# Expert picks on the logits, normed rows kept in place, the second bias on VectorE, alternating scatters, and one load for both results of a bin

## The chip, the cores and the metric

The kernel runs on one core of one Trainium2 chip. The metric is the device time of one execution in microseconds (us). Before the change the median of three runs is 2775.14 us (2773.34 to 2776.78).

## The reference, cut to what matters

Two layers, each added to its input, over 6250 nodes with 256 features, all in float32.

The graph layer norms the rows, builds one message for each of 100000 edges (two small products with a norm between them), sums the messages by source node and passes node and sum through two more products. The change does not touch its arithmetic.

The expert layer is what the change is about:

```python
tokens = layernorm(x)                                   # [6250, 256]
logits = tokens @ router_w.T                            # 8 experts
probs  = softmax(logits)
rw, re = top_k(probs, 2)
rw     = rw / max(rw.sum(-1), 1e-12)                    # two shares per token
for e in range(8):
    h   = gelu(tokens @ w1[e] + b1[e])
    y   = h @ w2[e] + b2[e]
    out = out + combine[:, e] * y                       # out starts as tokens
x = x + out
```

## The kernel before, in words

The nodes are cut into 50 bins of 126 rows (the last has 76). `node_rows` holds one bin per column block in SBUF: first the input, then the summed messages, then the running result. The program is a sequence of blocks, each of which gives every engine its own instruction list; a block ends when all engines have ended theirs.

- **nodes_and_sort** (to 600.5 us) norms the nodes, computes the products that do not depend on edges and sorts the edges. It zeroes `node_rows` on ScalarE (L564).
- **messages** (to 2151 us) goes over 838 tiles of 128 edges. The change touches it only in the shape of `node_rows` and by an instruction ahead of GpSimd's first one.
- A block between the two layers holds only GpSimd's `sem_clear` (L118).
- **update** (L1248) goes over the bins as a software pipeline written out by hand: a loop over steps `n` in every engine's list, in which an operation with lag `d` works on bin `n - d`. TensorE turns the sums of bin n (L1617), multiplies by `u1b` for bin n-2 (L1584), turns and multiplies again for bins n-3 and n-4, multiplies by the router for bin n-8 (L1605) and turns the normed row of bin n-7 (L1612). ScalarE copies the turned rows out of PSUM, applies Silu (L1539) and copies the logits last in its step (L1547). VectorE adds the u row (L1735), takes statistics (L1741, L1758), norms (L1751) into a ring `token` of 25 rows, adds xh (L1767) and adds token and x1 into `node_rows` (L1772). GpSimd makes the reciprocal deviation of one bin per step (`normal`, L1449, L1452). SyncE loads the u and xh rows four bins ahead (L1391, L1394) and, behind the fourth, both expert weights and the biases (L1397 to L1401).
- Routing goes by batches of five bins (the last two have three and two). In the step with lag 10 VectorE takes the batch's maximum and subtracts it (L1659, L1660) and ScalarE takes Exp (L1552); with lag 11 VectorE makes the softmax (L1667 to L1669) and the first pick (L1676 to L1684); with lag 12 the second pick, the counts (L1690, L1696) and the shares (L1705 to L1709); with lag 13 TensorE ranks (L1627, L1629); with lag 14 VectorE writes the places (L1719 to L1724). Then GpSimd scatters every normed row twice to the DRAM area `by_expert`, once for each pick: five `send` (L1464) for the first, in the five steps that follow, then five for the second. Each row carries the row number to which its result goes; GpSimd writes that number into `token` ahead of either half (`name_rows`, L1459), the second time after the first half has landed.
- **experts** (L1821) goes over 56 tiles of 256 scattered rows. TensorE's list has for each step the four transposes of tile n (L1940), the second product of tile n-4 into `ps_ye` and the first product of tile n-1. The second product is twice a bias matmul (`ones2` by `b2_parts`, two rows deep, L1953) and six matmuls (L1957). VectorE copies `ps_ye` out (L1989) and GpSimd scatters the two halves to `y_rows` (L1888). At the block's end GpSimd waits until all have landed.
- **combine** (L2016) is a block of its own: for each bin SyncE loads the two results with two transfers into a ring of eight bins (L2039), VectorE adds them with their shares into `node_rows` (L2055, L2062), ScalarE's queue stores the row (L2046).

What holds the order in the update, in a few lines (PE: the router's product; ScalarE; GpSimd's second half):

```python
pe.wait_ge(h2_t_ready, g + 1)
pe.wait_ge(l_kept, g)              # one PSUM buffer for the logits
product(ps_l[0:BIN, 0:E], h2_t[:, g % TURNED], rw).then_inc(l_ready, 1)

if i == size:
    pool.wait_ge(first_landed[b % 2], landed(b, 2))
    name_rows(b, 1)
```

Of the kernel before, what the change touches and what calls it, by code (L numbers as in the profile page):

```python
# [13 lines left out]
ds = bass.ds  # L14
# [37 lines left out]
ROUND = 1.5 * 2 ** 23  # L52

# [10 lines left out]
BATCHES = [(s, BATCH) for s in range(0, BINS - BATCH, BATCH)] + [(BINS - BATCH, 3), (BINS - 2, 2)]  # L64
HELD = 5 * BATCH
# [21 lines left out]
def gnn_ffn(nc, t, out):  # L87
    with ExitStack() as whole:
        whole.enter_context(nc.allow_non_contiguous_dma("small transposed parameters"))
        node_rows = whole.enter_context(nc.sbuf_tensor("node_rows", [P, BINS, D], F32))  # L90
# [8 lines left out]
        with ExitStack() as edges:  # L99
# [10 lines left out]
            messages(nc, dram, node_rows, ident, kept)  # L110
        dram["by_expert"] = nc.dram_tensor("by_expert", (EXPERTS * (REGION + MOE_TILE), XROW), F32).ap()
        dram["y_rows"] = nc.dram_tensor("y_rows", (2 * ROWS + 2 * EXPERTS * MOE_TILE, D), F32).ap()
        with ExitStack() as rest:
# [4 lines left out]
            with nc.Block() as block:  # L118
                @block.gpsimd
                def _(pool):  # L120

                    pool.sem_clear(range(used[0].num, used[-1].num + 1))

            tile_e = sb("tile_e", [1, MOE_TILES], I32)
            tile_off = sb("tile_off", [1, MOE_TILES], I32)
            with ExitStack() as weights:
# [8 lines left out]
                w["b2_parts"] = weights.enter_context(nc.sbuf_tensor("b2_parts", [2, EXPERTS, D], F32R))  # L135
                w["ones2"] = weights.enter_context(nc.sbuf_tensor("ones2", [2, P], F32R))
                update(nc, t, dram, node_rows, ident, w, shares, tile_e, tile_off)
                experts(nc, dram, ident, w, tile_e, tile_off)
            combine(nc, dram, node_rows, shares, out)


def nodes_and_sort(nc, t, dram, node_rows, ident, kept):
# [4 lines left out]
    with ExitStack() as ctx:  # L147
# [239 lines left out]
        def _(sp):  # L387
# [8 lines left out]
            sp.dma_start(node_rows[0:BIN, 0:BINS - 1, :],  # L396
                         t["x"][0:(BINS - 1) * BIN, :].rearrange("(b p) f -> p b f", p=BIN)).then_inc(x_in, 16)
            sp.wait_ge(last_clear, 1)
            sp.dma_start(node_rows[0:LAST, BINS - 1, :], t["x"][(BINS - 1) * BIN:, :]).then_inc(x_in, 16)
# [92 lines left out]
        def _(act):  # L492
# [71 lines left out]
            nc.scalar.activation(node_rows[:].rearrange("p b f -> p (b f)"), zero[:].broadcast_to([P, BINS * D]),  # L564
# [70 lines left out]
        def _(dve):  # L635
# [186 lines left out]
            for i in range(BINS):  # L822
                if i >= 2:
                    dve.wait_ge(means, i - 1)
                nc.vector.bn_stats(st6[0:BIN, i % 2, :], node_rows[0:BIN, i, :]).then_inc(stats, 1)
# [30 lines left out]
            def normed(i):  # L856
# [4 lines left out]
                nc.vector.tensor_scalar(h[0:BIN, i % 3, :], node_rows[0:BIN, i, :], mv[0:BIN, i, 0:1],  # L861
# [6 lines left out]
            for i in range(BINS):  # L868
# [7 lines left out]
                nc.vector.tensor_tensor(xh_out[0:BIN, k, :], h[0:BIN, i % 3, :], node_rows[0:BIN, i, :], ALU.add  # L876
# [69 lines left out]
def messages(nc, dram, node_rows, ident, kept):  # L946
# [6 lines left out]
    with ExitStack() as ctx:  # L953
# [72 lines left out]
        def _(pool):  # L1026
            nc.gpsimd.memset(half[:], -0.5).then_inc(start, 1)
# [146 lines left out]
        def _(dve):  # L1174
# [3 lines left out]
            def step(j, r, live):  # L1178
# [3 lines left out]
                def add_sums(i, d):  # L1182
# [4 lines left out]
                    sums = node_rows[0:BIN, ds(b[i], 1), :]  # L1187
# [60 lines left out]
def update(nc, t, dram, node_rows, ident, w, shares, tile_e, tile_off):  # L1248
# [5 lines left out]
    with ExitStack() as ctx:  # L1254
# [19 lines left out]
        token = sb("token", [P, HELD, XROW])  # L1274
        st6 = sb("st6_u", [P, R, 6])
        mv = sb("mv_u", [P, R, 2])
        rstd = sb("rstd_u", [P, R, 1])
        half = sb("half_u", [P, 1])
        blank = sb("blank", [P, E, 2, XROW])
        logits = sb("logits", [P, 2 * BATCH, E])  # L1280
# [6 lines left out]
        prob = sb("prob", [P, BATCH, E])  # L1287
        work = sb("work_r", [P, BATCH, E])
        low = sb("low", [P, BATCH])
        total = sb("total", [P, BATCH])  # L1290
        best = [sb("best0", [P, BATCH]), sb("best1", [P, BATCH])]
# [5 lines left out]
        b2 = sb("b2", [E, D])  # L1297
        b2_hi = sb("b2_hi", [E, D], F32R)
        b2_lo = sb("b2_lo", [E, D], F32R)
# [15 lines left out]
        b2_split = sem("b2_split")  # L1315
# [25 lines left out]
        exp_ready = sem("exp_ready")  # L1341
        route_step = sem("route_step")
# [3 lines left out]
        id_set = sem("id_set")  # L1346
        first_landed = [sem(f"first_landed{b}") for b in range(2)]
        second_landed = [sem(f"second_landed{b}") for b in range(HELD // BATCH)]
# [7 lines left out]
        STEPS = BINS + 30  # L1356
# [11 lines left out]
        def batch_of(g):  # L1368
# [6 lines left out]
        def due(g):  # L1375
            return 0 <= g < BINS
# [709 lines left out]
```

## Time and profile before

| what | us |
|---|---|
| median of three runs | 2775.14 |
| the profiled execution, own time | 2778.06 |
| its span, first to last instruction | 2776.3 |
| nodes and sort | 0 to 600.5 |
| messages | 600.5 to 2151 |
| update | 2152.5 to 2447.8 |
| experts | 2447.8 to 2710.3 |
| combine | 2710.3 to 2776.3 |
| busy: TensorE 2101.6, VectorE 2131.2, ScalarE 1683.1, GpSimd 1775.9 | |

The profiled execution is 2.9 us above the median; 1.8 us of its time lie outside the span. In the rows below, times are from the span's start; PE is TensorE's matmuls, PEld its weight loads, DVE VectorE, ACT ScalarE, POOL GpSimd, SPq the issue of a transfer by SyncE. The granted clock is a share of 2.4 GHz, so 0.50 is 1.2 GHz.

### The profile page before, as it was taken

The page shows a single profiled execution, that of the slowest core. Times are in us where ns is not written, and L with a number is a line of the kernel's source. Part 1 is how long each engine was busy: PE and PEld are TensorE (multiplying, and loading weights), DVE is VectorE, ACT ScalarE, POOL GpSimd, SP SyncE. Part 2 cuts the span into 40 slices and gives each one's busy share as a digit, 9 for nine tenths or more (in the row PEclk, how much of TensorE's full clock was granted, in tenths as well). Part 3 has the DMA queues.
Part 4 walks back from the last instruction along what each step waited for, and adds up shares of the span by engine and source line. Part 5 has one row for each costly group of instructions (what it writes and reads, how often), then busy time and mean ns, then how long its engine had stood idle before and what let it go on. Part 6 is the DMA issues. An engine that isn't in the chain of part 4 may idle for free. (4 is left out here: it accounts for less than half of the span.)

```text
span 2776.3 us, 63585 instructions
## 1 busy us (share of the span) xinstructions
PE 2101.6 (76%) x14268; PEld 1900.3 (68%) x14269; DVE 2131.2 (77%) x6895; ACT 1683.1 (61%) x3780; POOL 1775.9 (64%) x2320
## 2 busy tenths in 40 slices
PE   0000793039999999999999999999999788369980
PEld 0000682029999999999999999999998566258870
DVE  9993572229999999999999999999997477535546
ACT  5430120128888888888888888888886354145540
POOL 0007777568878878788788787887885256624440
PEclk9999996559999999999999999999999888679995
DMA  4000352012222222222222222222222533334428
GB/s 155 0 1 10 95 145 59 10 55 74 74 71 73 72 71 72 72 72 72 72 72 72 72 72 72 72 72 72 72 72 49 165 106 116 110 96 127 123 96 277
DMA packets 146161, 229.56 MB, mean 83 GB/s; under 512 B 33939, under 2 KB 102213, under 8 KB 145936
## 3 DMA queue, kind: packets, MB, share of 16 engines
q0 software_dynamic: 60672, 139.93, 17.3%
q1 hardware_dynamic: 76352, 80.66, 9.6%
q10 hardware_dynamic: 9040, 7.85, 0.9%
q8 instruction: 39, 0.64, 0.1%
q14 instruction: 58, 0.48, 0.1%
HBM read 166.37 MB, written 61.73 MB: 82 GB/s over the span
## 5 line engine op out<-in xcount | busy, mean ns | idle before, releaser
L1039 POOL DMA_INDIRECT rows<-b_rows,dst_row x838 | 840.0, 1002 | 231.9 <-issue 145.0
L1166 PE MATMUL ps_z<-w_hi,t_hi 128*128 128x256 f32 x1676 | 547.6, 327 | 0.0
L1167 PE MATMUL ps_z<-w_lo,t_hi 128*128 128x256 f32 x1676 | 468.5, 280 | 0.0
L1153 PE MATMUL ps_agg<-rows,onehot 128*126 128x256 f32 x1676 | 455.0, 394 | 17.5 <-DVE node_rows L1188 14.6
L1168 PE MATMUL ps_z<-w_hi,t_lo 128*128 128x256 f32 x1676 | 468.2, 279 | 0.0
L1072 ACT ACTIVATE rows<-rows,shift,rstd_m 128x256 f32<-128x256 f32 x838 | 452.5, 587 | 0.3 <-DVE shift L1196 0.3
L1188 DVE TENSOR_TENSOR node_rows<-node_rows,ps_agg 126x256 f32 x838 | 345.2, 412 | 106.2 <-issue 89.5
L466 POOL DMA_INDIRECT sorted_edges<-pay,place x245 | 242.9, 991 | 279.0 <-DVE place L808 199.4
L1099 ACT ACTIVATE rows<-rows 128x512 f32<-128x512 f32 x419 | 265.0, 633 | 189.1 <-DVE rows L1244 184.2
L1153 PEld LDWEIGHTS ps_agg<-rows,onehot 128*126 128x126 f32 x1676 | 281.5, 188 | 73.8 <-DVE node_rows L1188 23.0
L1049 POOL TENSOR_TENSOR rstd_m<-mv_m,half_m 128x2 f32<-128x2 f32 x419 | 305.8, 730 | 34.9
L1166 PEld LDWEIGHTS ps_z<-w_hi,t_hi 128*128 128x128 f32 x1676 | 316.4, 189 | 11.5
L1167 PEld LDWEIGHTS ps_z<-w_lo,t_hi 128*128 128x128 f32 x1676 | 316.5, 189 | 10.7
L1168 PEld LDWEIGHTS ps_z<-w_hi,t_lo 128*128 128x128 f32 x1676 | 315.1, 188 | 0.0
L1218 DVE BATCH_NORM_STATS2 st_m<-rows 128x6 f32<-128x256 f32 x838 | 312.5, 415 | 2.0 <-ACT rows L1099 1.9
L1228 DVE TENSOR_TENSOR t_lo<-ps_rt,t_hi 128x512 fp32r<-128x512 f32 x419 | 286.0, 683 | 0.2
L1244 DVE TENSOR_TENSOR rows<-rows,ps_pre 128x512 f32<-128x512 f32 x419 | 274.3, 655 | 12.6 <-DMA rows<-b_rows,dst_row 9.8
L1094 ACT ACTIVATE t_hi<-ps_rt 128x512 fp32r<-128x512 f32 x419 | 250.2, 597 | 21.2 <-PE ps_rt L1142 2.4
L1142 PE MATMUL ps_rt<-ident,rows 128*128 128x128 f32 x1676 | 253.8, 274 | 4.7 <-ACT rows L1072 4.6
L1121 PE MATMUL ps_pre<-a_hi,onehot_t 128*128 x838 | 241.5, 310 | 9.1 <-issue 5.3
L1078 ACT ACTIVATE rows<-ps_z 128x512 f32<-128x512 f32 x419 | 240.9, 575 | 6.8 <-PE ps_z L1168 6.5
L1123 PE MATMUL ps_pre<-a_lo,onehot_t 128*128 x838 | 220.3, 282 | 0.0
(315 smaller groups left out, 4503.4 us busy)
## 6 DMA issues: line engine op xcount, KB each, us to landing
x_e<-by_expert SPq DMA_DIRECT2D x56, 260.0 KB, 2.9
rows<-b_rows,dst_row POOLq DMA_INDIRECT x838
y_f<-y_rows SPq DMA_DIRECT2D x98, 126.0 KB
b_rows<-b_out SPq DMA_DIRECT2D x50, 126.0 KB
u_rows<-u_out SPq DMA_DIRECT2D x50, 126.0 KB
xh_rows<-xh_out SPq DMA_DIRECT2D x50, 126.0 KB
u_row_up<-u_rows SPq DMA_DIRECT2D x50, 126.0 KB
xh_row_up<-xh_rows SPq DMA_DIRECT2D x50, 126.0 KB
```

The lines of the kernel that those rows point to most:

```text
L1039: nc.gpsimd.indirect_dma_start(rows[r][:, i, :], None, dram["b_rows"], bass.IndirectOffsetOnAxis(ap=dst_row[:, r, i:i + 1], axis=0)).then_ ...
L1049: nc.gpsimd.tensor_tensor(rstd[:, q, :], mv[:, q, :, 1], half[:], ALU.pow).then_inc(rstd_ready, 1)
L1072: nm = nc.scalar.activation(rows[q][:, i, :], rows[q][:, i, :], ACT.Identity, bias=shift[:, q, i:i + 1], scale=rstd[:, q, i:i + 1])
L1099: nc.scalar.activation(x[:], x[:], ACT.Silu).then_inc(silu_ready, 1)
L1153: mm = pe.matmul(ps_agg[0:BIN, i * D:(i + 1) * D], onehot[:, q, i, 0:BIN], rows[q][:, i, :], start=True, stop=True)
L1166: pe.matmul(z, t_hi[:, k, i, c, :], w2_hi[:, c, :], start=(c == 0), stop=False)
L1167: pe.matmul(z, t_hi[:, k, i, c, :], w2_lo[:, c, :], start=False, stop=False)
L1168: mm = pe.matmul(z, t_lo[:, k, i, c, :], w2_hi[:, c, :], start=False, stop=(c == KC - 1))
L1188: nc.vector.tensor_tensor(sums, sums, ps_agg[0:BIN, i * D:(i + 1) * D] .rearrange("p (o f) -> p o f", o=1), ALU.add).then_inc(added, 1)
L1218: nc.vector.bn_stats(st6[:, i, :], rows[q][:, i, :]).then_inc(tile_stats, 1)
L1228: nc.vector.tensor_tensor(t_lo[:, k].rearrange("p i c e -> p (i c e)"), ps_rt[k][:], t_hi[:, k].rearrange("p i c e -> p (i c e)").bitcast( ...
L1244: nc.vector.tensor_tensor(x, x, ps_pre[q % 2][:], ALU.add).then_inc(pre_ready, 1)
```

## The change

`node_rows` gets four more columns (`XROW` = 260). The normed row is written into it in place and stays there; the ring `token` goes, and so does the add of L1772. The scatters read `node_rows`. The row numbers for both halves are made once (`ids`), and ScalarE copies them into column 256: all first numbers in step 8, the second numbers of a batch once its first half has landed. GpSimd's list then alternates: a first of batch b, then a second of batch b-1. `normal` works on two bins at once, every second step. The batches are 2, 3, eight times 5, 3 and 2, and routing starts one step earlier at its end (places with lag 13).

Picks are made on the logits, without softmax; the softmax, the shares and the base factor are computed once for all bins at the end of the update block. ScalarE copies the logits first in its step. The base (normed row plus x1, which is the normed row times a factor plus the mean) is made in place by ScalarE in the experts block, one bin per tile, with Identity. The expert weights are split in every second step instead of every step.

The bias matmuls go; `b2` is loaded broadcast to all partitions (1024 KB instead of 8 KB, at the same place in SyncE's list), and VectorE adds it where it copied before. The combine moves into the experts block: SyncE waits there until the scatters have landed and loads both results of a bin with one transfer. The block with `sem_clear` goes; the clear stands ahead of GpSimd's list in messages.

The diff, cut to its core:

```diff
-BATCHES = [(s, BATCH) for s in range(0, BINS - BATCH, BATCH)] + [(BINS - BATCH, 3), (BINS - 2, 2)]
+SIZES = [2, 3] + [BATCH] * 8 + [3, 2]
+BATCHES = [(sum(SIZES[:b]), size) for b, size in enumerate(SIZES)]
...
-            with nc.Block() as block:
-                    pool.sem_clear(range(used[0].num, used[-1].num + 1))
...
 update, SyncE
-                    sp.dma_start(b2[:], t["L0_ffn_b2"]).then_inc(biases_in, 16)
+                    sp.dma_start(w["b2"][:], t["L0_ffn_b2"].rearrange("(o e) n -> o e n", o=1).broadcast_to([P, E, D])
...
 update, GpSimd
             def normal(g):
-                hold(pool, stats_ready, g + 1)
+                hold(pool, stats_ready, g + 2)
...
+            def send_second(b, i):
+                if i == 0:
+                    hold(pool, second_named, b + 1)
+                send(BATCHES[b][0] + i, 1, second_landed)
+
             for n in range(STEPS):
-                if due(n - 5):
-                    normal(n - 5)
+                if due(n - 6) and n % 2 == 0:
+                    normal(n - 6)
...
                 for b, (s, size) in enumerate(BATCHES):
-                    i = n - (s + size - 1 + 14)
+                    i = n - (s + size - 1 + SEND)
...
-                    if i == size:
-                        pool.wait_ge(first_landed[b % 2], landed(b, 2))
-                        name_rows(b, 1)
...
+                    send(s + i, 0, first_landed[b % 2])
+                    if b:
+                        count = BATCHES[b - 1][1]
+                        for j in range(count):
+                            if j == i - 1 or (i == size - 1 and j >= i):
+                                send_second(b - 1, j)
...
 update, ScalarE
+                g = n - 9
+                if due(g):
+                    act.wait_ge(l_ready, g + 1)
+                    nc.scalar.activation(logits[0:BIN, g, :], ps_l[0:BIN, 0:E], ACT.Copy).then_inc(l_kept, 1)
                 g = n - 1
...
-                b = batch_at(n, 10)
-                    act.wait_ge(shifted, b + 1)
-                    nc.scalar.activation(p, p, ACT.Exp).then_inc(exp_ready, 1)
+                b = batch_at(n, SEND + BATCH)
+                    act.wait_ge(first_landed[b % 2], landed(b, 2))
+                    nc.scalar.activation(node_rows[0:BIN, s:s + size, D:D + 1].bitcast(I32),
+                                         ids[0:BIN, 1, s:s + size].rearrange("p (b o) -> p b o", o=1), ACT.Copy
+                                         ).then_inc(second_named, 1)
...
 update, VectorE
-                    nc.vector.tensor_scalar(token[0:BIN, g % HELD, 0:D], x1[0:BIN, q, :], mv[0:BIN, q, 0:1],
+                    nc.vector.tensor_scalar(node_rows[0:BIN, g, 0:D], x1[0:BIN, g % R, :], mv[0:BIN, g, 0:1],
...
-                    nc.vector.tensor_tensor(node_rows[0:BIN, g, :], token[0:BIN, g % HELD, 0:D], x1[0:BIN, g % R, :],
-                                            ALU.add).then_inc(sum_ready, 1)
-                b = batch_at(n, 14)
+                b = batch_at(n, 13)
                     set_places(b)
-                b = batch_at(n, 12)
+                b = batch_at(n, 11)
                     pick(b, 1)
                     count(b)
-                    set_shares(b)
-                b = batch_at(n, 11)
-                    softmax(b)
-                    pick(b, 0)
                 b = batch_at(n, 10)
-                    shift_logits(b)
+                    pick(b, 0)
...
 experts
+            for r in range(X):
+                sp.wait_ge(y_sent[r], 32 * len(range(r, T, X)))
+            for n in range(BINS):
+                if n >= F:
+                    sp.wait_ge(second_added, n - F + 1)
+                both = dram["y_rows"][0:2 * ROWS, :].rearrange("(k b p) n -> b p k n", k=2, p=BIN)
+                sp.dma_start(y_back[0:rows(n), n % F, :, :], both[n, 0:rows(n)]).then_inc(y_in[n % F], 16)
...
-            for r in range(X):
-                pool.wait_ge(y_sent[r], 32 * len(range(r, T, X)))
...
+                    nc.scalar.activation(node_rows[0:BIN, n, 0:D], node_rows[0:BIN, n, 0:D], ACT.Identity,
+                                         bias=spread["mv"][0:BIN, n, 0:1], scale=spread["gain"][0:BIN, n:n + 1]
+                                         ).then_inc(base_ready, 1)
...
-                        pe.matmul(to, w["ones2"][:], w["b2_parts"][:, ds(e, 1), :].rearrange("p o n -> p (o n)"),
-                                  start=True, stop=False)
...
-                    nc.vector.tensor_copy(y[:, k % Y].rearrange("p i n -> p (i n)"), ps_y[k % 2][:]
-                                          ).then_inc(y_kept, 1)
+                    nc.vector.tensor_tensor(y[:, k % Y], ps_y[k % 2][:].rearrange("p (i n) -> p i n", i=2),
+                                            w["b2"][:, ds(expert(dve, k), 1), :].broadcast_to([P, 2, D]), ALU.add
+                                            ).then_inc(y_kept, 1)
```

## Rows read from the trace of the kernel before

**Rows 1.** Busy time by stretch: us, PE, PEld, DVE, ACT, POOL, clock, DMA share, GB/s

```profile
2460.00:2700.00 240.00, 235.01 (x1640) 203.93 (x1638) 131.02 (x217) 128.24 (x272) 108.47 (x112) 1.00 0.38 116
2720.00:2770.00 50.00, 0.00 (x0) 0.00 (x0) 37.33 (x86) 0.00 (x0) 0.00 (x0) 0.50 0.95 330
```

**Rows 2.** Timeline, first and last scatters: start us, length, engine, line, instruction

```profile
2228.71 1.12 POOL L1464 DMA_INDIRECT by_expert<-token_up,place_up  x1 [2.56 <-DVE place_up L1724]
...
2230.97 1.07 POOL L1464 DMA_INDIRECT by_expert<-token_up,place_up  x1 [0.23 <-issue]
...
2388.56 0.98 POOL L1464 DMA_INDIRECT by_expert<-token_up,place_up  x1 [0.30 <-issue]
...
2389.84 0.98 POOL L1464 DMA_INDIRECT by_expert<-token_up,place_up  x1 [0.30 <-issue]
...
2435.50 0.99 POOL L1464 DMA_INDIRECT by_expert<-token_up,place_up  x1 [0.30 <-issue]
2447.84 49.20 SPq L1880 DMA_DIRECT2D x_e<-by_expert  x15
```

**Rows 3.** Timeline, VectorE, one long step of the update (second pick, counts, shares)

```profile
2347.20 0.42 DVE L1735 TENSOR_TENSOR act_up<-ps_v,u_row_up 126x256 f32<-126x256 f32 x1
...
2348.73 0.41 DVE L1772 TENSOR_TENSOR node_rows<-token_up,x_up 126x256 f32<-126x256 f32 x1
...
2349.06 0.19 DVE L1676 TENSOR_REDUCE best_up<-prob_up 126x5 f32<-126x40 f32 x1
...
2351.34 0.15 DVE L1705 TENSOR_TENSOR total_up<-best_up 126x5 f32<-126x5 f32 x1
...
2352.34 0.42 DVE L1735 TENSOR_TENSOR act_up<-ps_v,u_row_up 126x256 f32<-126x256 f32 x1
```

**Rows 4.** Timeline, VectorE, a step without routing: two adds that follow each other

```profile
2188.76 0.42 DVE L1735 TENSOR_TENSOR act_up<-ps_v,u_row_up 126x256 f32<-126x256 f32 x1 [0.93 <-PE ps_v L1574]
...
2191.81 0.42 DVE L1735 TENSOR_TENSOR act_up<-ps_v,u_row_up 126x256 f32<-126x256 f32 x1 [1.05 <-PE ps_v L1574]
```

**Rows 5.** Waits of PE, 2186 to 2375 us: total us, times, longest

```profile
PE ps_l L1574 <- ACT logits_up L1547: 26.8, 23, 2.5
```

**Rows 6.** Timeline, VectorE: the fifth bin's add

```profile
2179.77 0.42 DVE L1735 TENSOR_TENSOR act_up<-ps_v,u_row_up 126x256 f32<-126x256 f32 x1 [10.63 <-DMA u_row_up<-u_rows]
```

**Rows 7.** Transfers by line: count, KB each, median us from issue to landing

```profile
w_raw<-in_L_ffn_w SPq DMA_DIRECT2D x2, 2048.0 KB, 15.3
...
y_rows<-y_e,x_e POOLq DMA_INDIRECT x112, 2.9
```

**Rows 8.** Timeline, PE: the end of one bias group and the start of the next

```profile
2668.28 0.28 PE L1957 MATMUL ps_ye<-w_lo_e,g_hi 128*128 x1
2668.40 0.28 PE L1957 MATMUL ps_ye<-w_hi_e,g_lo 128*128 x1
2668.61 0.38 PE L1953 MATMUL ps_ye<-b_parts,ones 2*128 x1
2668.92 0.39 PE L1957 MATMUL ps_ye<-w_hi_e,g_hi 128*128 x1
2669.14 0.28 PE L1957 MATMUL ps_ye<-w_lo_e,g_hi 128*128 x1
```

**Rows 9.** Groups by line in the experts, 2460 to 2700 us

```profile
L2003 DVE TENSOR_TENSOR x_lo<-ps_x,x_hi 128x512 fp32r<-128x512 f32 x53 | 36.6, 691 | 38.2 <-ACT x_hi L1909 38.2
...
L1902 ACT ACTIVATE w_hi_tile<-w_hi_e 128x512 fp32r x53 | 33.4, 631 | 97.7 <-PE ps_h L1974 97.7
```

**Rows 10.** Groups by line of ScalarE, whole span

```profile
L1072 ACT ACTIVATE rows<-rows,shift,rstd_m 128x256 f32<-128x256 f32 x838 | 452.5, 587 | 0.3 <-DVE shift L1196 0.3
...
L1552 ACT ACT_TABLE_LOAD x9 | 11.5, 1283 | 0.2
```

**Rows 11.** Timeline from the last scatter of results to the first load of the combine

```profile
2698.23 0.97 POOL L1888 DMA_INDIRECT y_rows<-y_e,x_e  x1 [0.30 <-DMA y_rows<-y_e,x_e]
2710.35 6.05 SPq L2039 DMA_DIRECT2D y_f<-y_rows  x14
```

More of the change, by code:

```diff
@@ L52 @@
 ROUND = 1.5 * 2 ** 23
+FAR = 3e38
 ROWS = BINS * BIN
@@ L134, in gnn_ffn @@
                 w["b1"] = weights.enter_context(nc.sbuf_tensor("b1", [P, KC, EXPERTS], F32))
[L135 to L139, printed above, removed]
+                w["b2"] = weights.enter_context(nc.sbuf_tensor("b2", [P, EXPERTS, D], F32))
+                update(nc, t, dram, node_rows, ident, w, shares, spread, tile_e, tile_off)
+                experts(nc, dram, node_rows, ident, w, shares, spread, tile_e, tile_off, out)
 def nodes_and_sort(nc, t, dram, node_rows, ident, kept):
@@ L1026, in _ @@
         def _(pool):
+            pool.sem_clear(range(used[0].num, used[-1].num + 1))
             nc.gpsimd.memset(half[:], -0.5).then_inc(start, 1)
@@ L1273, in update @@
         h2_t = sb("h2_t", [P, TURNED, KC, BIN])
-        token = sb("token", [P, HELD, XROW])
         st6 = sb("st6_u", [P, R, 6])
-        mv = sb("mv_u", [P, R, 2])
-        rstd = sb("rstd_u", [P, R, 1])
-        half = sb("half_u", [P, 1])
+        ids = sb("ids", [P, 2, BINS])
+        mv, gain = spread["mv"], spread["gain"]
+        rstd = sb("rstd_u", [P, BINS])
+        half = sb("half_u", [P, 2])
         blank = sb("blank", [P, E, 2, XROW])
-        logits = sb("logits", [P, 2 * BATCH, E])
+        logits = sb("logits", [P, BINS, E])
         pcol = sb("pcol", [P, 1])
@@ L1426, in _ @@
             nc.gpsimd.memset(half[:], -0.5).then_inc(consts, 1)
+            for k in range(2):
+                nc.gpsimd.iota(ids[:, k, :], [[BIN, BINS]], base=k * ROWS, channel_multiplier=1,
+                               allow_small_or_imprecise_dtypes=True).then_inc(consts, 1)
             nc.gpsimd.iota(before[:], [[1, P]], base=0, channel_multiplier=-1, allow_small_or_imprecise_dtypes=True
@@ L1682, in pick @@
                 if k == 0:
[L1684 removed]
+                    then(nc.vector.scalar_tensor_tensor(out=left[0:BIN, 0:size, :], in0=h, scalar=-FAR, in1=rows,
+                                                        op0=ALU.mult, op1=ALU.add))
             def count(b):
@@ L1862, in experts, with rows @@
         y_kept = sem("y_kept")
+        y_in = [sem(f"y_in{r}") for r in range(F)]
+        base_ready = sem("base_ready")
+        first_added = sem("first_added")
+        second_added = sem("second_added")
+        stored = sem("stored")
         y_sent = [sem(f"y_sent{r}") for r in range(X)]
         block = ctx.enter_context(nc.Block())
+        def rows(n):
+            return BIN if n < BINS - 1 else LAST
         def due(k):
```

293 lines of the change are left out of this document (120 added, 173 removed).

## The prediction, made before the changed kernel was run

> **What bounds the kernel now.** I read the busy time by stretch first, to see which resource is full in each stage; then the timeline of the stage ends, to see who comes last; then the waits and groups inside. Three of the five stages are touched.
>
> In the experts TensorE is busy 235 us of 240 at a granted clock of 1.00, and in the combine the DMA engines are busy 0.95 of the time at 330 GB/s [rows 1]. So the experts shrink only by what leaves TensorE, and the combine only by bytes or by DMA time. The update ends with GpSimd's queue: the last of its 100 scatters starts at 2435.50, and they follow each other at 1.28 us (2388.56, 2389.84); the experts' first load follows 12.3 us after the last one starts [rows 2]. The first starts only at 2228.71, 76 us into the stage. Behind GpSimd stands VectorE: a step with routing lasts 5.14 us (add at 2347.20, next add at 2352.34), one without 3.05 [rows 3, 4].
>
> **Update.** The first scatter needs the first batch's places. Before, that is a batch of five with lag 14, so step 18; now a batch of two with lag 13, so step 14. Four steps at the mean of the two kinds, (5.14 + 3.05)/2 = 4.1 [rows 3, 4], are -16.4. `b2` grows from 8 to 1024 KB behind two transfers of 2048 KB that land after 15.3 us [rows 7], and the fifth bin's add already waits 10.63 us for a u row queued behind these [rows 6]: 1024/4096 of 15.3 is +3.8 (bounds 0, if it overlaps with the free step behind it, and 7.6, if a broadcast moves at half that rate). The logits copy comes first in ScalarE's step; TensorE waited 26.8 us in 23 steps for it [rows 5], 1.2 each. Most of that is refilled by the chain through VectorE, so I take a quarter, 0.3 in each of the eight steps before the first batch is complete: -2.4 (bounds 0 and -9.6). First scatter: 2228.71 - 16.4 + 3.8 - 2.4 = 2213.7.
>
> From there GpSimd has 100 scatters at 1.28, 128 us, and 21 pair norms. One norm between two scatters makes their distance 2.26 instead of 1.28 [rows 2], so 0.98 each, 20.6. Were it never to wait it would end at 2362.3. It does wait: batches of 2 and 3 are sent in about 13 us (10 scatters), the first batch of five is complete eight steps, some 25 us at 3.05 [rows 4], behind the first: 11.5; and I give each of ten later batches 0.7, half a scatter, 7. End 2380.8. The other way: per batch of five VectorE loses the second pick's shares (2351.34 to 2352.34, 1.00) and five adds of L1772 at 0.33 (2348.73 to 2349.06) [rows 3], besides the softmax of lag 11; I estimate 16 us of VectorE a batch against 15.5 of GpSimd (ten scatters, 2.5 norms), nearly level, which ends some 3 us later. I take the last scatter's start at 2381.5: **-54**. Bounds: -74, GpSimd never waiting; and -31, steps no quicker than now and only the loop shorter, by six steps (BINS + 30 to BINS + 24) of 5.14 [rows 3].
>
> New waits: ScalarE waits for a batch's first half to land before it writes the second numbers. A scatter lands 2.9 us after its issue [rows 7]; the last first-scatter of a batch is issued one step before, so up to 1 or 2 us a batch, behind which stand the Silu and the turning copies and so TensorE's next products. VectorE's longer lag (norm in step g + 7 behind a pair norm) covers it; uncovered it is 10 x 2 = 20, inside the bound above. GpSimd no longer waits there but for ScalarE's copy, one scatter into the batch, with the rest of its scatters queued behind. The norms of two bins come every second step, so the first of a pair waits a step longer; the lags allow that step and no second one. The softmax, shares and factors for all bins at the end run on VectorE and ScalarE under the last scatters, some twenty instructions on 400 columns at most; the cover is the twelve scatters after the last places, 15 us. Were it gone, I'd pay as for one second half of a long step, 5.14. The removed block (`sem_clear`) goes ahead of GpSimd's work in the messages, whose first inputs come later: 0. Zeroing four more columns in 256 is 1.6% of one ScalarE instruction: 0.
>
> **Experts.** In PE's timeline the bias matmul starts at 2668.61 and the next at 2668.92: 0.31 for the bias alone. From the matmul before (2668.40) over the bias to the second after it (2669.14) are 0.74, where three ordinary distances of 0.12 to 0.22 would be 0.50 without it [rows 8]. The two per tile thus cost 2 x 0.31 = 0.62 by one reading; a bias of other depth also breaks the overlap of weight load and matmul around it, so I take 2 x 0.41 = 0.83, between 0.62 and 0.94 (2 x 0.47, all of 0.74 but the two shortest distances). 52 tiles in steady state: **-43** (bounds -32 and -49). What could take TensorE's place: VectorE's add replaces a copy of the same 128x512, and the like subtraction takes 0.69 [rows 9]. ScalarE gets one Identity per tile; on 128x256 that is 0.587 [rows 10], and in the experts ScalarE waits 97.7 us over 53 tiles for TensorE, 1.84 a tile [rows 9], so it fits: 0. Expected period 4.28 - 0.83 = 3.45.
>
> **Drain.** From the last result scatter to the first load of the combine are 12.1 us [rows 11], a block end included. Now SyncE waits only for the landing, 2.9 [rows 7], and some 0.9 for the issue: **-8.3** (bounds -5 and -9.2). The same gap ahead of the experts stays.
>
> **Combine.** Same bytes in half the transfers, DMA already at 0.95 [rows 1]: 0 (-3 to +3; 5% of 66 us is 3.3). In the rows, the DMA share says that at most those 3.3 us are spent on anything but moving. The Trainium skill, "DMA: Bandwidth & Descriptors", would have a fixed cost of some 2 us for each transfer and asks for large ones; fifty transfers fewer would by that be 100 us if they ran one by one. The row speaks against it: they overlap, and I keep 0.
>
> **Sum.** -54 - 43 - 8.3 = -105.3, from the profiled execution's 2778.06: 2672.8. That execution is 2.9 above the median, so **2670**.
>
> **The rivals.**
> - *Steps stay tied.* If TensorE's, VectorE's and ScalarE's turn-taking sets the step rather than VectorE's load, the update gains -31: 2693. For it: TensorE's waits for ScalarE [rows 5], and the new wait on landings. Against: the long steps carry the work that goes [rows 3]. 0.17.
> - *GpSimd never waits*: -74, 2650. For it: scatters at 1.28 back to back [rows 2]. Against: the small batches run dry. 0.12.
> - *The experts' tile shrinks by 0.4 only*, since VectorE's and ScalarE's chain between the two products is next: 52 x 0.43 = 22 less, 2692. Against it are the 38.2 and 97.7 us that they wait now [rows 9]. 0.07.
> - *The merged load helps* by the 5% that the DMA engines are idle [rows 1], 3.3: 2667. 0.03.
> - *Table loads.* ACT_TABLE_LOAD takes 1.283 [rows 10]. If Identity beside Gelu costs two a tile, ScalarE's tile is 2.44 (4.28 less 1.84) + 0.59 + 2.57 = 5.60 against 3.45; 50 tiles are +108, 2778: no gain. No row shows Identity beside Gelu. 0.01. The Trainium skill, "ScalarE: Activation LUTs", says that the cheap functions are in every set; no run shown here tells.
> - *Slower: TensorE's clock in the experts.* It is granted 1.00 (2.4 GHz) there while busy 235 of 240 us, and 0.50 (1.2 GHz) in the combine where it is idle [rows 1]. A leaner tile with more idle time between groups might be granted 0.50. TensorE's tile is 235/56 - 0.83 = 3.37; at half clock 6.74, 3.29 over the period of 3.45. It eats the whole gain of 105 from 32 of the 56 tiles on; all 56 would give 2670 + 184 = 2854. Against it: by the sum TensorE stays busy 3.37 of 3.45. 0.02.
>
> **How the numbers follow.** The forecast as summed has 0.58, with its own range from 2645 to 2697 (unknown costs partly cancelling). All bounds at once give 2640 and 2709; the other cases with weight lie between 2650 and 2693. I give 2643 to 2704. Within 0.2% (5.5 us, about what a measurement of this kernel tells from no change) only the table loads come: 0.01; slower only the clock: 0.02; faster 0.97.
>
> **What would show it.** Right: the first scatter near 2214 and the last near 2381, at about 1.28 with gaps only in the first 25 us; a period of 3.45 between the first products of neighbouring tiles, without rows of two-partition matmuls, clock 1.00; no ACT_TABLE_LOAD inside the experts; 4 us between the last result scatter and the first load back; a DMA share of 0.95 in the last 66 us. Wrong: GpSimd waiting for `place` or for ScalarE's names in every batch (update), ScalarE waiting long for landings with TensorE idle behind it, VectorE's `y` add on the path (experts), or u rows landing over 4 us later than now behind `b2`.

## The result and the profile after

The changed kernel takes 2671.93 us (median of four runs, 2667.65 to 2676.7) against 2775.96 us for the kernel before in the same runs: a ratio of 0.9627, with a 95% interval from 0.9608 to 0.9645. The forecast was 2670, with a range from 2643 to 2704. The profiled execution has a span of 2668.8 us, 107.5 less than the 2776.3 of before.

The stage ends first. From the timelines of GpSimd and SyncE of the changed kernel (start us, length, engine, line, instruction), the first and the last scatter of the update, the first load of the experts, the last scatter of results and the first load of the combine:

```profile
2208.41 1.10 POOL L1454 DMA_INDIRECT by_expert<-node_rows,place_up  x1 [1.30 <-issue]
...
2380.51 0.99 POOL L1454 DMA_INDIRECT by_expert<-node_rows,place_up  x1 [0.30 <-issue]
2381.80 1.14 POOL L1454 DMA_INDIRECT by_expert<-node_rows,place_up  x1 [0.30 <-issue]
...
2394.76 23.54 SPq L1863 DMA_DIRECT2D x_e<-by_expert  x9
...
2600.26 0.96 POOL L1880 DMA_INDIRECT y_rows<-y_e,x_e  x1 [0.30 <-issue]
...
2602.75 1.30 SPq L1873 DMA_DIRECT2D y_back<-y_rows  x3
```

Set beside [rows 2, 11], these give the following table. Each stretch is measured from its own start; the update starts with its first load, at 2152.48 before and 2150.18 after.

| stretch | before | after | difference | forecast |
|---|---|---|---|---|
| update, first load to the experts' first load | 295.4 | 244.6 | -50.8 | -54 |
| experts, first load to last scatter of results | 250.4 | 205.5 | -44.9 | -43 |
| last scatter of results to first load back | 12.1 | 2.5 | -9.6 | -8.3 |
| combine, to the end | 65.9 | 66.1 | +0.1 | 0 |
| start of the update | 2152.5 | 2150.2 | -2.3 | 0 |

The last line can't be laid to the change: over the twelve other changed kernels below, none of which touches anything ahead of the update, that start lies between 2149.0 and 2154.9 us.

The update itself splits at two instructions of VectorE, the adds of the fifth and of the last bin:

```profile
2178.77 0.43 DVE L1701 TENSOR_TENSOR act_up<-ps_v,u_row_up 126x256 f32<-126x256 f32 x1 [12.37 <-DMA u_row_up<-u_rows]
...
2329.56 0.42 DVE L1701 TENSOR_TENSOR act_up<-ps_v,u_row_up 126x256 f32<-126x256 f32 x1
```

Before, they stand at 2179.77 [rows 6] and at 2367.80. The fill (stage start to the fifth add) is 27.3 before and 28.6 after; the **loop** from there to the last bin's add 188.0 and 150.8; the **tail** from there to the last scatter 67.7 and 52.2, in which 39 scatters follow each other at 1.29 us (2380.51, 2381.80); and from there to the experts 12.3 and 13.0. So the loop gave 37.2 us and the tail 15.5.

The busy times by stretch show what each stage is near (us, PE, PEld, DVE, ACT, POOL, granted clock, DMA share, GB/s; loop of the update, experts, combine):

```profile
2215.00:2315.00 100.00, 90.79 (x564) 76.03 (x563) 78.35 (x301) 51.92 (x170) 66.50 (x81) 1.00 0.49 143
2425.00:2590.00 165.00, 160.57 (x1342) 156.43 (x1341) 114.45 (x191) 133.95 (x281) 106.77 (x97) 1.00 0.51 152
...
2612.00:2662.00 50.00, 0.00 (x0) 0.00 (x0) 36.72 (x85) 0.00 (x0) 0.00 (x0) 0.50 0.95 326
```

The same stretch of the loop in the kernel before:

```profile
2215.00:2315.00 100.00, 79.77 (x413) 61.99 (x413) 75.29 (x295) 49.91 (x138) 55.55 (x87) 0.89 0.34 103
```

TensorE ran 564 matmul records there instead of 413, and its granted clock is 1.00 (2.4 GHz) instead of 0.89. It is the fullest engine of the loop, and still of the experts, at 1.00 as in [rows 1]. The combine's row is taken as far behind its first load as that in [rows 1], and its DMA share is 0.95 in both. In the experts' groups (2405 to 2590 us; line, engine, operation, busy us, mean ns, idle before), VectorE's add costs what the copy cost before (0.691 us on average against 0.692), and what was slack in [rows 9] is partly used:

```profile
L2001 DVE TENSOR_TENSOR x_lo<-ps_x,x_hi 128x512 fp32r<-128x512 f32 x53 | 36.6, 692 | 39.0 <-ACT x_hi L1898 38.4 <-issue 0.7
L1986 DVE TENSOR_TENSOR y_e<-ps_ye,b 128x512 f32<-128x512 f32 x53 | 36.6, 691 | 12.1 <-issue 8.4 <-PE ps_ye L1953 2.0
...
L1891 ACT ACTIVATE w_hi_tile<-w_hi_e 128x512 fp32r x53 | 33.5, 632 | 29.1 <-PE ps_h L1971 29.1
...
L1920 ACT ACTIVATE node_rows<-node_rows,mv_x,gain_x 126x256 f32<-126x256 f32 x48 | 29.0, 605 | 0.0
...
L1915 ACT ACT_TABLE_LOAD x1 | 1.3, 1283 | 0.0
```

ScalarE's wait for TensorE fell from 97.7 to 29.1 us, its Identity (L1920) costs 0.605, and one table load stands in the whole block.

### The profile page after: what moved, and what is told of

Read it like the earlier page. It is cut to its first block and busy times, and to the rows that moved or that the text cites. A ratio compares the mean times of both kernels' runs of the same rounds, so it can differ in the third digit from the quotient of the medians.

```text
span 2668.8 us, 63199 instructions
## 1 busy us (share of the span) xinstructions
PE 2025.3 (76%) x14160; PEld 1864.4 (70%) x14161; DVE 2099.3 (79%) x6765; ACT 1692.5 (63%) x3817; POOL 1770.6 (66%) x2247
```

## The experiments

All twelve are the changed kernel with one edit, but for two that combine several, each timed beside the kernel before. Differences to the changed kernel are worked out as (ratio - 0.9627) x 2776; each ratio's interval is about 0.002 to either side, so a difference under some 7 us isn't told by the times alone, and the rows decide there. Rows have a spread of their own: four kernels with the same code in the update (the changed one, those with two loads and with a block of its own for the combine, and the ring of nine) have loops of 148.7 to 150.9 us and last scatters 229.4 to 232.6 us after the stage's start.

**The bias back on TensorE.**

```diff
-                    nc.vector.tensor_tensor(y[:, k % Y], ps_y[k % 2][:].rearrange("p (i n) -> p i n", i=2),
-                                            w["b2"][:, ds(expert(dve, k), 1), :].broadcast_to([P, 2, D]), ALU.add
+                    nc.vector.tensor_copy(y[:, k % Y].rearrange("p i n -> p (i n)"), ps_y[k % 2][:]
...
+                        pe.matmul(to, w["ones2"][:], w["b2_parts"][:, ds(e, 1), :].rearrange("p o n -> p (o n)"),
+                                  start=True, stop=False)
...
-                    sp.dma_start(w["b2"][:], t["L0_ffn_b2"].rearrange("(o e) n -> o e n", o=1).broadcast_to([P, E, D])
+                    sp.dma_start(b2[:], t["L0_ffn_b2"]).then_inc(biases_in, 16)
```

> The second bias goes back to TensorE: two matmuls two rows deep per tile, VectorE copies where it added, b2 is loaded as 8 KB. If the bias matmuls are what the experts lost, first load to last result scatter grows from 204 us to about 250 and the whole time from 2671.9 to about 2717 (+46); TensorE's period per tile goes from 3.28 to about 4.2. The smaller load should make the fifth bin's add come 1 to 4 us earlier in the update. If the experts' gain came from something else in the block (the loads, the base on ScalarE, the slower splitting of weights), the time grows by under 20.

Measured 2714.1 us, ratio 0.9777 (0.9759 to 0.9796): +42. First load to last result scatter is 251.2 us, and between the first and the last scatter of results a tile takes 4.19 us where the changed kernel takes 3.37 and the kernel before 4.18 (each is that stretch over 55.5 tiles). The bias matmul shows in PE's timeline:

```profile
2501.86 0.38 PE L1969 MATMUL ps_ye<-b_parts,ones 2*128 x1
2502.17 0.39 PE L1973 MATMUL ps_ye<-w_hi_e,g_hi 128*128 x1
...
2502.86 0.28 PE L1973 MATMUL ps_ye<-w_hi_e,g_lo 128*128 x1
2503.07 0.38 PE L1969 MATMUL ps_ye<-b_parts,ones 2*128 x1
2503.38 0.39 PE L1973 MATMUL ps_ye<-w_hi_e,g_hi 128*128 x1
2503.60 0.28 PE L1973 MATMUL ps_ye<-w_lo_e,g_hi 128*128 x1
```

From the last matmul ahead of the bias (2502.86) to the second one behind it (2503.60) are 0.74 us. The same stretch of the changed kernel, without the bias, is 0.23:

```profile
2502.51 0.28 PE L1953 MATMUL ps_ye<-w_hi_e,g_lo 128*128 x1
...
2502.74 0.28 PE L1953 MATMUL ps_ye<-w_lo_e,g_hi 128*128 x1
```

So this bias costs TensorE 0.51 us, and the experts' gain is the bias matmuls. The fifth bin's add comes 25.6 us after the stage's start instead of 28.6: the broadcast costs some 3.0 us of the fill (2.4 to 3.9 beside the nine kernels here that load b2 in the same place, with fills of 28.0 to 29.5).

**Two loads per bin.**

```diff
-                sp.dma_start(y_back[0:rows(n), n % F, :, :], both[n, 0:rows(n)]).then_inc(y_in[n % F], 16)
+                for k in range(2):
+                    at = k * ROWS + n * BIN
+                    sp.dma_start(y_back[0:rows(n), n % F, k, :], dram["y_rows"][at:at + rows(n), :]
+                                 ).then_inc(y_in[n % F], 16)
```

> Only the merged load is undone: a bin's two results come with two transfers again, inside the same block. By the prediction 0 (-3 to +3): the last 66 us are a matter of bytes. If the merged load saves a cost per transfer, at least +3.3, all of it between the first load back and the end.

Measured 2674.21 us, ratio 0.9631 (0.9613 to 0.9649), and 65.8 us from the first load back to the end against 66.1. The merged load gives nothing here. The Trainium skill, "DMA: Bandwidth & Descriptors", "Rules for kernel authors", asks to join many small transfers into one large one. No run of this case shows a gain from that, at a DMA share of 0.95.

**The combine in its own block.** The edit ends the block behind the last scatter and begins a new one for the loads, adds and stores.

> The combine is a block of its own again, with the merged load. By the prediction +8.4: last result scatter to first load back grows from 3.75 to about 12.1, nothing else moves. If the 8.4 us belonged to the merged load or to the scatters' landing and not to the end of a block, under +3.

Measured 2681.7 us, ratio 0.966 (0.9643 to 0.9676): +9. From the timelines of GpSimd and SyncE:

```profile
2605.42 0.96 POOL L1874 DMA_INDIRECT y_rows<-y_e,x_e  x1 [0.30 <-DMA y_rows<-y_e,x_e]
...
2617.52 2.74 SPq L2016 DMA_DIRECT2D y_back<-y_rows  x6
```

12.1 us, against 2.5 in one block: the gap belongs to the end of the block and the start of the next.

**Batches of five from the start.**

```diff
-SIZES = [2, 3] + [BATCH] * 8 + [3, 2]
+SIZES = [BATCH] * 9 + [3, 2]
```

> Batches of 5, 5, ..., 3, 2 as before instead of 2, 3, 5, ...; all else as changed. By the prediction's working the last scatter follows the first one, so a first scatter three steps later (about +9) moves the end by about +9 (2681). The rival, from the trace of the changed kernel: GpSimd has 33 scatters without a wait at the end and 26 us of waits ahead of them, so the end hangs on the last bins alone and the early scatters only fill waits: 0 (-2 to +2) while the first scatter comes 9 us later.

Measured 2673.06 us, ratio 0.9634 (0.9618 to 0.965): no difference. GpSimd's timeline:

```profile
2216.53 1.12 POOL L1454 DMA_INDIRECT by_expert<-node_rows,place_up  x1 [4.27 <-issue]
...
2378.57 1.14 POOL L1454 DMA_INDIRECT by_expert<-node_rows,place_up  x1 [0.30 <-issue]
```

The stage starts at 2149.02 in this kernel, so the first scatter comes 67.5 us after it instead of 58.2, and the last one 229.6 instead of 231.6, which is within the spread. A first scatter 9 us later does not move the end. So the early scatters fill GpSimd's waits, and the end hangs on the last bins.

**Firsts, then seconds.**

```diff
+                    if 0 <= i - BATCH < size:
+                        send_second(b, i - BATCH)
...
-                        for j in range(count):
-                            if j == i - 1 or (i == size - 1 and j >= i):
-                                send_second(b - 1, j)
```

> All firsts of a batch, then all its seconds five steps behind, as before, in place of first, second of the batch before, first and so on. GpSimd then needs the second names in the step in which ScalarE waits for the last first to land (2.9 us). If the alternation is what hides the landing, GpSimd waits 2 to 3 us in every batch; in the middle that falls into its idle time, at the end it counts for the last four or five batches: +10 (5 to 15). If other scatters lie between in any case: 0 to +2.

Measured 2695.73 us, ratio 0.9699 (0.9677 to 0.972): +20, twice what was expected. GpSimd's timeline in the tail (last bin's add at 2345.03):

```profile
2365.05 0.98 POOL L1454 DMA_INDIRECT by_expert<-node_rows,place_up  x1 [0.30 <-issue]
2368.96 0.99 POOL L1454 DMA_INDIRECT by_expert<-node_rows,place_up  x1 [2.92 <-ACT node_rows L1533]
...
2383.53 0.99 POOL L1454 DMA_INDIRECT by_expert<-node_rows,place_up  x1 [0.30 <-issue]
2388.34 0.99 POOL L1454 DMA_INDIRECT by_expert<-node_rows,place_up  x1 [3.83 <-ACT node_rows L1533]
...
2404.02 1.15 POOL L1454 DMA_INDIRECT by_expert<-node_rows,place_up  x1 [0.30 <-issue]
```

The two waits make up most of the 6.8 us by which the tail is longer (59.0). The other 12 us lie in the loop (162.9 against 150.8), which the expectation left out: ScalarE waits there for the same landings (14.3 us in the loop, 8.0 in that of the changed kernel), and the steps behind them last 7.2, 7.8 and 7.8 us (from one bin's add to the next, bins 32, 37 and 47 counted from 0) where the changed kernel has 3.6, 3.1 and 3.7.

**The logits copied last.** The four lines at the head of ScalarE's step move behind Silu.

> ScalarE copies the logits last in its step again. If TensorE sets the steps of the update (busy 89 of 98 us in the middle), its wait for this copy counts: about 0.3 us in each of 40 steps, +12 (5 to 20). If VectorE or the scatters set them, 0 to +2.

Measured 2679.81 us, ratio 0.9642 (0.9621 to 0.9663): +4, not clear from zero by the times. By the rows the loop is 155.0 us, 4.2 longer, and outside the spread; it is less than was expected. TensorE does wait 9.6 us in 13 steps for this copy, but its waits for VectorE's norm and for ScalarE's turning copy, 12.7 us in the changed loop, fall to 0.3.

**VectorE's load added back.**

```diff
+                    nc.vector.tensor_tensor(scrap[0:BIN, :], x1[0:BIN, g % R, :], x1[0:BIN, g % R, :], ALU.add)
...
+                    for _ in range(8):
+                        then(nc.vector.tensor_tensor(scrap_r[0:BIN], index[0:BIN], index[0:BIN], ALU.add))
```

> VectorE gets about the work back that the change took from it, as adds into buffers that nobody reads: one 126x256 add per step and eight 126x40 adds per batch, some 3.5 us per five steps, 37 us in all. If VectorE's long steps held the update, +20 to +37. If VectorE has slack now (busy 76 of 98 us in the middle) and the steps are set by TensorE's chain, under +8.

Measured 2708.35 us, ratio 0.9751 (0.9726 to 0.9776): +34. The loop lasts 181.6 us. Its busy times between the fifth and the last add, in the kernel before, the changed one and this one:

```profile
2180.00:2368.00 188.00, 157.78 (x823) 122.33 (x824) 135.13 (x527) 92.45 (x261) 101.25 (x166) 0.90 0.38 115
```

```profile
2179.00:2330.00 151.00, 137.60 (x832) 114.94 (x832) 112.33 (x440) 74.36 (x245) 85.35 (x109) 0.98 0.48 144
```

```profile
2180.00:2361.00 181.00, 149.93 (x832) 124.23 (x832) 139.70 (x553) 74.83 (x245) 86.72 (x110) 0.92 0.41 121
```

VectorE's busy time (the third column behind the length) is 135.1, 112.3 and 139.7. The change took 22.8 us from it; this kernel adds 27.4 and the loop grows by 30.8. VectorE is busy in only 112 of the changed loop's 151 us, and yet the added time counts in full. Two rows go with it. TensorE's granted clock is lower, 0.92 instead of 0.98 (0.90 before), and it is busy 149.9 us instead of 137.6 with the same 832 matmuls. And it waits 29.0 us for VectorE's norm instead of 8.0; first the changed kernel's wait, then this one's, over the same stretches (total us, times, longest):

```profile
PE ps_ht L1559 <- DVE node_rows L1711: 8.0, 11, 1.4
```

```profile
PE ps_ht L1561 <- DVE node_rows L1713: 29.0, 16, 3.4
```

**Weights late.**

```diff
-                if n == R - 1:
-                    for m, name in enumerate(("L0_ffn_w1", "L0_ffn_w2")):
-                        sp.dma_start(w["raw"][m][:], t[name].rearrange("e (c p) n -> p e c n", p=P)
-                                     ).then_inc(w["in"], 16)
+                i = (n - 14) // 2 if n >= 14 and n % 2 == 0 else 2 * E
+                if i < 2 * E:
...
+                    sp.dma_start(w["raw"][i % 2][:, i // 2],
+                                 t[("L0_ffn_w1", "L0_ffn_w2")[i % 2]][i // 2].rearrange("(c p) n -> p c n", p=P)
+                                 ).then_inc(w_part[i % 4], 16)
```

> The expert weights come in 16 transfers of 256 KB, one with every second bin from the 14th on, and the biases behind them, instead of 5 MB at once ahead of the fifth bin's u row. The fifth add's wait of 12.4 us goes, and part of the 3.1 us at the tenth. If the fill of the pipeline counts in full, the first and the last scatter come about 12 us earlier: 2660 (-12, between -9 and -15). If the later transfers slow the u rows and the scatters in the middle, or ScalarE waits for them, less: -5 to +5.

Measured 2671.8 us, ratio 0.9604 (0.9581 to 0.9627): -6, half of what was expected and not clear from zero. The fifth add does come 17.1 us after the stage's start instead of 28.6, and the first scatter 13 us earlier, but the loop takes 157.4 us instead of 150.8. Part of that stands in ScalarE's wait for landings between 2200 and 2330:

```profile
ACT node_rows L1544 <- DMA by_expert<-node_rows,place_up: 13.2, 5, 4.0
```

In the changed kernel it is 8.0 in the same window. With the weights late the steps to bins 42 and 47 last 6.5 and 7.2 us, where the changed kernel has 4.7 and 3.7.

**Splits behind the loop.**

```diff
-            i = n - 20
-            return i // 2 if 0 <= i < 4 * E and i % 2 == 0 else None
+            i = n - 51
+            return i if 0 <= i < 2 * E else None
```

> The 16 splits of the expert weights (0.68 us of VectorE and 0.6 of ScalarE each) move from steps 20 to 50 to steps 51 to 66, behind the last bin's u row, where VectorE stands mostly idle under GpSimd's last 39 scatters. If VectorE's load counts in full in the loop, as 37 us added made it about 32 us longer, the last bin's add and the last scatter come 8 to 11 us earlier: 2662. If the steps that carry a split have slack (they wait 1.05 to 1.65 us for TensorE), 0 to -3.

Measured 2671.06 us, ratio 0.962 (0.96 to 0.9639): no difference. The loop lost only 2.1 us (148.7), which is within the spread, though 9 us of VectorE's busy time left it, and the last scatter comes 230.4 us after the start instead of 231.6. The step to bin 42 lasts 6.3 us instead of 4.7, and ScalarE's wait for landings (8.7 us between 2200 and 2330) is there as before. In the loop it is now TensorE that has little time left (138.4 busy us of 149), and VectorE's adds wait 27.2 us for its product between 2180 and 2329, where they wait 22.1 us in the changed loop:

```profile
2179.00:2328.00 149.00, 138.41 (x832) 116.24 (x832) 103.48 (x423) 66.34 (x229) 83.95 (x108) 0.97 0.49 147
```

So VectorE's time, which counted in full when it was added, is not seen to count when it is taken away from the changed kernel.

**A ring of nine tiles.** `X, Y, R, F = 8, 4, 4, 8` becomes `9, 4, 4, 8` in the experts.

> The ring of loaded tiles in the experts is 9 deep instead of 8. In seven profiles of the same experts block the stretch from first load to last result scatter was 205 to 212 us, with TensorE waiting 2 to 5 us for a tile's load. If the loads' lead is now what is next in the experts, these waits go and the stretch is 203 or less: -2 to -7. If the differences come from something else, the stretch stays between 205 and 212.

Measured 2664.74 us, ratio 0.9598 (0.9582 to 0.9614): -8. The stretch is 198.7 us. In PE's waits of the changed kernel between 2425 and 2590 (total us, times, longest) stands

```profile
PE ps_x L1938 <- DMA x_e<-by_expert: 2.0, 3, 0.8
```

and with nine tiles there is none, at 163.47 busy us of 165:

```profile
2425.00:2590.00 165.00, 163.47 (x1387) 163.07 (x1386) 118.37 (x196) 136.22 (x286) 115.42 (x101) 1.00 0.51 156
```

The three kernels with nine tiles took 198.7, 198.4 and 198.4 us for the stretch, the nine with eight tiles and no bias matmul 205.5 to 211.9. So the ring was what came next in the experts. A tile's place in it comes free only when its two result scatters, which read their row numbers there, have landed, and SyncE waits for this in 44 of the changed kernel's loads between 2425 and 2590:

```profile
SPq L1861 <- DMA y_rows<-y_e,x_e: 102.8, 44, 4.3
```

TensorE's own wait for a load explains only 2.0 of the 6.9 us; where the rest stood isn't shown.

**Late weights, late splits, nine tiles.** The last three edits together, the weights with every second bin from the 10th on (the 14th above) and waited for once.

> Splits behind the loop, ring of 9, and the weights in 16 transfers of 256 KB with every second bin from the 10th on, all waited for once ahead of the first split. Terms: fill -11.5 (the fifth add waited that much less with late weights), splits -8 to -11, ring -2 to -7; but ScalarE's wait for landings in every batch takes back some 5 of the fill, as it did with late weights alone: 2652 (2643 to 2662). If GpSimd's 15.5 us per batch become the bound, the end stays where splits_late puts it.

Measured 2650.0 us, ratio 0.9542 (0.9526 to 0.9558): 24 us below the changed kernel and the fastest here. From the timelines of VectorE, GpSimd and SyncE, the fifth add, the last scatter and the first load of the experts:

```profile
2167.99 0.42 DVE L1703 TENSOR_TENSOR act_up<-ps_v,u_row_up 126x256 f32<-126x256 f32 x1 [0.66 <-PE ps_v L1566]
...
2367.19 1.14 POOL L1456 DMA_INDIRECT by_expert<-node_rows,place_up  x1 [0.30 <-issue]
...
2380.80 1.51 SPq L1865 DMA_DIRECT2D x_e<-by_expert  x2
```

The update takes 229.6 us instead of 244.6: fill 16.8, loop 145.2. Alone, the late splits leave the update at 244.9 us and the late weights at 239.8; together they take 15 us from it. The rows show where each alone lost its gain, and not why the two do more together. With the weights alone the fill is as short, and the loop loses it again in the steps to bins 42 and 47; together these last 3.8 and 3.5 us. With the splits alone the loop is hardly shorter, and the tail and the gap to the experts grow by 1.4 and 1.5 us. Together, TensorE's granted clock in the loop is 1.00, and it is busy 135.8 of 145.2 us. My reading is that the earlier first scatter lets GpSimd keep up with a shorter loop; no run tests it.

**The second names one step later.**

```diff
-                b = batch_at(n, SEND + BATCH)
+                b = batch_at(n, SEND + BATCH + 1)
...
-                            if j == i - 1 or (i == size - 1 and j >= i):
+                            if j == i - 2 or (i == size - 1 and j >= i - 1):
```

> late_ring9 with ScalarE's copy of the second names one step later, and the seconds one place later in GpSimd's list to match. In late_ring9 ScalarE waits 10.6 us in six of these steps for a landing (2200 to 2330), and the steps behind them are longer (3.9 us at bins 27 and 37 where 2.7 to 3.0 is usual). If these waits are on the path, the copy finds the rows landed, the last bin's add comes some 5 us earlier (3 to 8) and the time is about 2645. If the waits are filled by other work, or only move to GpSimd, 0 to -1 and 2650.

Measured 2654.51 us, ratio 0.9569 (0.9554 to 0.9585): no gain, and rather a loss beside the kernel above (0.9542). The wait for landings (7.9 us between 2200 and 2315) is gone from ScalarE, but the first of these grew from 13.0 us and the other two are new:

```profile
ACT agg_t_up L1511 <- PE ps_at L1561: 18.2, 35, 1.6
...
DVE node_rows L1713 <- POOL rstd_u_up L1451: 3.3, 5, 1.2
POOL by_expert L1456 <- ACT node_rows L1541: 2.2, 1, 2.2
```

From bin 22's add (counted from 0) to the last one 87.7 us pass instead of 89.0, so 1.3 of the 8 us of waits came back. The way to that add is 3.0 us longer, of which GpSimd's new wait for the names shows 2.2, and one scatter more is left for the tail.

## Why the prediction was right, and where it wasn't

- **Update, -54 forecast, -50.8 measured.** The sum had two ways to its end, and only one held. The first, "First scatter: 2213.7", with GpSimd's queue counted from there, was wrong as a mechanism: with batches of five the first scatter comes 9 us later and the last one does not. It came out near because its terms compensated: the first scatter 5 us earlier on the span's clock than forecast, GpSimd's waits longer (173.4 us from first to last scatter, 167.8 forecast). The step that failed is "from there GpSimd has 100 scatters": it counted the last scatter from the first, with waits of a fixed size (11.5 and 7), while in the runs GpSimd's waits take up what the first one gains or loses. The other way, 16 us of VectorE a batch, came nearer: the loop takes 150.8 / 9 = 16.8 us per five bins. But of these VectorE is busy in 12.5 and TensorE in 15.3, so it is the chain of the two that fits, and not VectorE's load alone.
- **What made the loop shorter.** VectorE's 22.8 us less, at the 1.12 us that the experiment lost per us added (30.8/27.4), would be 26 of the 37. That is an estimate, since taking away need not pay what adding costs, and the clock is in it: TensorE's own time in the loop fell from 157.8 to 137.6 us. The order of the scatters is worth 12 in the loop and 7 in the tail, the logits 4. These add up to more than the 37, so they overlap. A rival for a share of it was not tried apart: 16 table loads, 20.5 us of ScalarE, left the loop. In the kernel before they stand on the way from VectorE's add to the Silu that needs it:

```profile
2274.73 0.42 DVE L1735 TENSOR_TENSOR act_up<-ps_v,u_row_up 126x256 f32<-126x256 f32 x1 [0.30 <-PE ps_v L1574]
...
2275.51 1.28 ACT L1539 ACT_TABLE_LOAD   x1
2276.81 0.42 ACT L1539 ACTIVATE act_up<-act_up 126x256 f32<-126x256 f32 x1
```

- **The order of the scatters.** The alternation was the large part that the sum had no term for: it was priced only as a wait for landings that VectorE's longer lag "covers". Undone, it costs 20 us, the price that the prediction gave for this wait uncovered. The wait is there in the changed kernel too, 11.0 us in six steps between 2208 and 2345:

```profile
ACT act_up L1527 <- DVE act_up L1701: 29.9, 34, 2.1
POOL by_expert L1454 <- issue: 28.6, 68, 4.0
...
ACT node_rows L1539 <- DMA by_expert<-node_rows,place_up: 11.0, 6, 3.0
```

- **The tail,** 15.5 us shorter, has no term in the sum. Two waits of GpSimd's in the kernel before, between 2368 and 2436, explain most of it: for its own writing of the row numbers, and for the landings ahead of that. In the changed kernel's tail neither is there, and it holds 39 scatters instead of 41.

```profile
POOL by_expert L1464 <- POOL token_up L1459: 6.8, 8, 0.9
POOL token_up L1459 <- DMA by_expert<-token_up,place_up: 4.8, 3, 2.0
```

- **The broadcast b2, +3.8 forecast:** some 3.0 on the changed kernel by the bias run. The logits' copy, -2.4: 4.2 by its run, but in the loop and not ahead of the first batch.
- **Experts, -43 forecast, -44.9 measured.** Right in place, and undone by the bias alone. The size, 4.18 to 3.37 us a tile or 0.81 against the 0.83 taken, came near in part by luck. The bias was read too small. The prediction sets three ordinary distances against the 0.74 us over it, and without the bias there are two, of 0.23 together, so that the one shown costs 0.51 and not 0.41. Nor does the upper bound of 0.47 come out of [rows 8], whose shortest distance, 0.12, taken twice leaves 0.50. With nine tiles, where no tile is waited for, a tile takes 3.24, 0.94 less than before. The ring of eight, which the prediction did not name, took 7 us of that back (up to 13 in the other kernels with this experts block, where the experts would have gained 38.5). The period of 3.45 started from 4.28, too high by 0.10 beside the 4.18 measured.
- **Drain, -8.3 forecast, -9.6 measured,** beyond its bound of -9.2, and +9.6 when the block is cut again. The last scatters land after 2.4 us, where the median of 2.9 was taken, and the load follows 0.1 us behind, where 0.9 was taken. **Merged load, 0:** the combine's time and its DMA share of 0.95 are those of before.
- **The rivals.** Steps that stay tied would have given 2693. They are indeed tied, but the tied steps became shorter, where this rival had them no quicker than before. GpSimd never waiting: it does wait between 2208 and 2345. Of the 28.6 us under "issue" above, 0.30 ahead of each of 68 scatters are their usual distance, which leaves 8 us; 12.8 more it waits for VectorE's statistics. Table loads: one in the experts beside 48 Identities, so the rival is out; the Trainium skill, "ScalarE: Activation LUTs", "Table sets: the hidden batching unit", has the cheap functions in every set, and this trace agrees. TensorE's clock in the experts stayed at 1.00.

## What to carry to other kernels

When two estimates of one stage end near each other, find out which of them holds before adding their parts: an early start only helps a queue that never runs dry. In a loop where engines take turns, an engine with a quarter of its time idle can still cost a microsecond for each microsecond added, and yet give nothing back when more is taken from it. After taking out the bound, look for the next wait of few microseconds (here one more buffer for the tiles, 8 us): two edits that give nothing or little alone gave 15 together here.

## What was not expected of the hardware

- The end of a block with scatters in flight and the start of the next cost 9.6 us more than a wait for the landings inside one block (12.1 against 2.5, both from the last scatter to the next load).
- TensorE's granted clock in the loop of the update was 0.90 before, 0.98 after, and 0.92 with VectorE work added and nothing else changed. TensorE's own time for the same matmuls rose by 12 us (137.6 to 149.9), beside the 31 us by which the loop grew.
- The same experts block took 205.5 to 211.9 us in nine kernels in which TensorE waits 2.0 to 5.4 us for its tiles' loads, and 198.4 to 198.7 in three with one more buffer and no such wait: the spread went with the waits.
